# One core, cross attention with top-32 and a quantised feed-forward: the instruction order of all five engines written anew

## The chip, the core and the metric

The kernel runs on one NeuronCore of a Trainium2 chip. The metric is the device time of one execution in microseconds (us); less is better. The engines are named as in the profile: PE is TensorE (matmuls), PEld its weight loads, DVE is VectorE, ACT is ScalarE, POOL is GpSimd, and SP issues most of the DMAs. Each engine works through its own list of instructions in the order in which they are written and meets the others through semaphores alone, so an instruction that waits holds up all that stands behind it on its engine.

## What is computed

```python
x = x + xattn(layernorm(x), ctx_1024, top_k=32)       # x: 2048 x 256, ctx: 1601 x 256
x = x + ffn(layernorm(x))                             # 256 -> 1024 -> 256

# xattn: q = query @ Wq.T + bq;  k, v from ctx in the same way
scores = q @ k.T / sqrt(256)                          # 2048 x 1601
# all but the 32 largest scores of each row become -inf
ctx = softmax(scores) @ v;  out = ctx @ Wo.T + bo

# ffn: bitlinear, exact gelu, bitlinear
xq = act_quant(rmsnorm(x))    # rows to whole numbers -128..127, by the row's largest |x|
wq = weight_quant(w)          # -1, 0, 1, by the mean of |w|
h  = xq @ wq.T + b
```

## The kernel before

The 2048 rows are 16 tiles of 128, t = 0 to 15. Two neighbouring tiles form a pair, j = 0 to 7, and share a set of query transposes and quantisation scales. The 1601 context rows are cut into four column chunks c = 0 to 3 (400, 400, 400, 401) for the scores and into 13 blocks of 128 for the transposes; these blocks are handled in four groups q = 0 to 3 (4, 4, 4 and 1 blocks).

A head of about 43 us turns the context, folds the weight matrices together, projects keys and values, and makes the feed-forward weights ternary. Then each tile passes through these steps (names of the code's functions; each is one or a few instructions):

- PE `scores(t, c)`: 6 matmuls into PSUM bank `score<c>`; ACT `copy_scores(t, c)` copies it to `s_sb`. The four score banks exist once, so `scores(t+1, c)` waits for `copy_scores(t, c)`.
- DVE `candidates(t, c)` (8 MAX8 instructions), then `best_8` and three `next_8` (`drop_8` and `best_8`): the 32nd largest score. The first `best_8` also yields `neg_max`, on which ACT `exp_all(t)` waits. DVE `count(t)` tests whether the candidates suffice; SP `turn_counts(t)` brings its result into one row by DMA, DVE `largest_count(t)` reads it. DVE `weigh(t)` zeroes what is below the 32nd. `release(t)` reads the test's result in DVE's sequencer, branches, and gives the tile to PE.
- PE `turn_weights(t, q)` transposes into one of two banks (TURN), ACT `take_weights(t, q)` copies to `pT`, PE `weighted(t, q)` multiplies by the values. DVE `attended(t)` normalises and adds the residual, `moments(t)` and `centre(t)` are the second layer norm.
- POOL `row_scales_1(j)` (seven tiny steps) and `quantise_1(j, u)`, PE `turn_y1(j)`, ACT `take_y1(j)`, PE `up(t, h)` for the halves h = 0, 1, ACT `hidden(t, h)`, POOL `add_bias(t, h)`, ACT `gelu(t)` and `squares(t)`, DVE `gelu_max(t)`, POOL `row_scales_2(j)`, ACT `quantise_2(t)` and `lower_2(t)`, a transposing DMA `turn_y2(t)` on SP, PE `down(t)`, DVE `output(t)`, SP `store(t)`.

The last tiles go through variants of one tile or half a tile (`turn_y1_tile`, `gelu_half`, `tile_scales_1`, `tile_scales_2`, `quantise_half`) with DVE doing some of ACT's and POOL's steps; `hold_clock(23)` is 23 transposes whose result nobody reads. Tiles overlap: while PE does the attention of tile t, it also does scores of t+2 or t+3, `up` of the pair before and `down` of the one before that. ACT's exp and gelu need different function tables, and an ACT_TABLE_LOAD stands between them.

What sets the order is code written out by hand: each engine's body calls these functions one after another, in the middle of the kernel in a loop over rounds r (one pair each), so that every round has the same order. `s_sb`, `e_all`, `pT`, `cand` have two buffers (t modulo 2), x2 and cen four.

## Time and profile before

| | |
|---|---|
| device time, median of 3 runs | 279.48 us (278.39, 279.48, 279.64) |
| span of the profiled execution, first to last instruction | 277.2 us |
| median less span | 2.3 us |
| PE busy | 262.5 us (95%) |
| DVE busy | 230.2 us (83%) |
| ACT busy | 215.8 us (78%) |
| POOL busy | 165.0 us (60%) |
| PE idle from 42 to 219 us | 177.00 less 173.37: 3.6 us |
| PE idle from 219 us to the end | 58.2 less 48.7: 9.5 us |

The page gives no device time for the profiled execution itself; its span stands beside the runs' median. A busy time is the union of an engine's instructions. PE's matmuls overlap in the records (one lasts longer than the distance to the next), so PE's rate is read from the distances between starts, and a wait of 0.2 us is not seen as idle at all.

### The profile page before, as it was taken

The page shows a single profiled execution, that of the slowest core. Times are in us where ns is not written, and L with a number is a line of the kernel's source. Part 1 is how long each engine was busy: PE and PEld are TensorE (multiplying, and loading weights), DVE is VectorE, ACT ScalarE, POOL GpSimd, SP SyncE. Part 2 cuts the span into 40 slices and gives each one's busy share as a digit, 9 for nine tenths or more (in the row PEclk, how much of TensorE's full clock was granted, in tenths as well). Part 3 has the DMA queues.
Part 4 walks back from the last instruction along what each step waited for, and adds up shares of the span by engine and source line. Part 5 has one row for each costly group of instructions (what it writes and reads, how often), then busy time and mean ns, then how long its engine had stood idle before and what let it go on. Part 6 is the DMA issues. An engine that isn't in the chain of part 4 may idle for free. (4 is left out here: it accounts for less than half of the span.)

```text
span 277.2 us, 5366 instructions
## 1 busy us (share of the span) xinstructions
PE 262.5 (95%) x1527; PEld 230.4 (83%) x1527; DVE 230.2 (83%) x984; ACT 215.8 (78%) x323; POOL 165.0 (60%) x235
## 2 busy tenths in 40 slices
PE   7999999999999899999999999999999999799784
PEld 7999998998887788988898889888978898577463
DVE  2561868988979897989898989899989798989894
ACT  2567495586589988988799879987998899647762
POOL 3334409931888587849775887678767943612330
PEclk9999999999999999999999999999999999999999
DMA  6991010046000330025001500151004100610011
GB/s 223 316 342 40 4 38 0 1 79 151 2 2 0 77 78 0 0 69 125 0 4 45 139 5 4 38 140 18 0 1 124 31 1 2 151 38 5 0 38 38
DMA packets 29436, 16.42 MB, mean 59 GB/s; under 512 B 20445, under 2 KB 28190, under 8 KB 29406
## 3 DMA queue, kind: packets, MB, share of 16 engines
q1 hardware_dynamic: 28702, 15.02, 20.3%
q0 software_dynamic: 272, 0.79, 1.0%
q10 hardware_dynamic: 432, 0.26, 0.3%
q8 instruction: 12, 0.20, 0.3%
q14 instruction: 18, 0.15, 0.2%
HBM read 9.77 MB, written 2.10 MB: 43 GB/s over the span
## 5 line engine op out<-in xcount | busy, mean ns | idle before, releaser
L399 PE MATMUL bank<-vo,pT 128*128 128x257 f32 (+1 forms) x416 | 97.1, 381 | 2.4 <-ACT pT L1101 2.4
L399 PEld LDWEIGHTS bank<-vo,pT 128*128 128x128 f32 (+1 forms) x416 | 76.0, 190 | 15.1 <-ACT pT L1101 4.8
L1413 DVE MAX8 cand<-s_sb 128x8 f32<-128x50 f32 (+1 forms) x512 | 60.0, 201 | 1.6 <-issue 1.1
L258 PE MATMUL score<-k_high,q_low 128*128 128x400 f32 (+1 forms) x128 | 49.5, 387 | 0.0
L868 POOL TENSOR_TENSOR g<-g,b_bc 128x512 f32<-128x512 f32 x24 | 37.9, 1592 | 12.1 <-ACT g L1125 12.1
L258 PE MATMUL score<-k_low,q_high 128*128 128x400 f32 (+1 forms) x128 | 44.2, 346 | 0.0
L258 PE MATMUL score<-k_high,q_high 128*128 128x400 f32 (+1 forms) x128 | 44.0, 344 | 0.0
L1052 ACT ACTIVATE s_sb<-score 128x400 f32<-128x400 f32 x64 | 30.6, 504 | 10.2 <-PE score L258 10.1
L1101 ACT ACTIVATE pT<-bank 128x512 f32<-128x512 f32 x64 | 31.9, 514 | 4.2 <-PE bank L266 4.2
L1448 DVE SCALAR_TENSOR_TENSOR e_all<-s_sb,best,e_all 128x1601 f32<-128x1601 f32 x16 | 34.2, 2138 | 0.9 <-ACT e_all L1093 0.5
L266 PE MATMUL bank<-ident,e_all 128*128 128x128 f32 (+1 forms) x208 | 30.7, 273 | 2.6 <-ACT pT L1101 2.6
L1093 ACT ACTIVATE e_all<-s_sb,neg_max 128x1601 f32<-128x1601 f32 x16 | 26.1, 1629 | 4.5 <-DVE neg_max L1426 4.5
L266 PEld LDWEIGHTS bank<-ident,e_all 128*128 128x128 f32 (+1 forms) x208 | 24.4, 140 | 5.6 <-issue 3.6
L764 POOL TENSOR_SCALAR xn<-x_in,ln_mv,ln_r 128x256 f32<-128x256 f32 x16 | 27.8, 1741 | 0.9
L258 PEld LDWEIGHTS score<-k_high,q_low 128*128 128x128 f32 x128 | 24.1, 189 | 2.4
L258 PEld LDWEIGHTS score<-k_low,q_high 128*128 128x128 f32 x128 | 24.2, 189 | 0.7
L258 PEld LDWEIGHTS score<-k_high,q_high 128*128 128x128 f32 x128 | 24.1, 189 | 0.0
L1609 DVE TENSOR_REDUCE g_max<-g 128x1 f32<-128x1024 f32 x14 | 17.0, 1218 | 7.6 <-ACT g L1135 7.6
L1423 DVE MAX8 best<-cand 128x8 f32<-128x64 f32 (+1 forms) x64 | 20.8, 325 | 2.0
L822 POOL TENSOR_SCALAR row<-ln_mv 128x2 f32<-128x2 f32 x7 | 1.3, 192 | 28.8 <-issue 15.4
L1135 ACT ACTIVATE g<-g 128x1024 f32<-128x1024 f32 x14 | 14.9, 1067 | 3.7 <-POOL g L868 3.7
L1125 ACT ACTIVATE g<-bank,row 128x512 f32<-128x512 f32 x24 | 15.8, 685 | 2.3 <-PE bank L430 2.1
(162 smaller groups left out, 503.2 us busy)
## 6 DMA issues: line engine op xcount, KB each, us to landing
x_in<-in_x SPq DMA_DIRECT2D x16, 128.0 KB, 2.2
w_sb<-in_L_ffn_w SPq DMA_DIRECT2D x2, 1024.0 KB, 12.1
x_res<-in_x SPq DMA_DIRECT2D x16, 128.0 KB, 2.9
out<-o_sb SPq DMA_DIRECT2D x16, 128.0 KB, 2.0
ctx_sb<-in_ctx SPq DMA_DIRECT2D x2, 512.0 KB, 7.6
ctx_sb<-in_ctx SPq DMA_DIRECT2D x2, 256.0 KB, 4.1
b_bc<-in_L_ffn_b POOLq DMA_DIRECT2D x1, 512.0 KB, 7.6
w_q<-in_L_xattn_Wq SPq DMA_DIRECT2D x1, 256.0 KB, 2.8
```

The costliest lines, as they stand in the source:

```text
L258: ins = pe.matmul(out, a, b, start=(i == 0), stop=(i == len(steps) - 1))
L266: ins = pe.transpose(bank[0:src.shape[1], at:at + rows], src, ident[0:rows, 0:rows])
L399: ins = pe.matmul(bank[:, 0:DV], pT[0:n, t % 2, b * P:(b + 1) * P], vo[0:n, b, :], start=(b == 0), stop=(b == SB - 1))
L764: pool.tensor_scalar(xn[:, u, :], x_in[:, u, :], ln1_mv[:, u, 0:1], ln1_r[:, 1, u:u + 1], ALU.subtract, ALU.mult).then_inc(xn_ready, 1)
L868: pool.tensor_tensor(g[:, t % 2, part], g[:, t % 2, part], b1_bc[:, part], ALU.add).then_inc(biased, 1)
L1052: act.activation(s_sb[:, t % 2, at:at + n], score[c][:, 0:n], ACT.Copy).then_inc(s_copied, 1)
L1093: act.activation(e_all[:, t % 2, :], s_sb[:, t % 2, :], ACT.Exp, bias=neg_max[:, t % 2:t % 2 + 1], scale=SCALE).then_inc(e_ready, 1)
L1101: drain(act.activation(pT[0:rows, t % 2, lo * P:hi * P], bank(("p", t, q))[0:rows, 0:(hi - lo) * P], ACT.Copy), ("p", t, q))
L1413: ins = dve.max(cand[:, t % 2, k:CAND:PIECES], s_sb[:, t % 2, k * PIECE:end])
L1423: dve.max(best[:, u, k, :], cand[:, u, 0:DEPTH[k] * PIECES]).then_inc(topk_step[u], 1)
L1448: dve.scalar_tensor_tensor(e_all[:, u, :], s_sb[:, u, :], least_kept(t), e_all[:, u, :], ALU.is_ge, ALU.mult).then_inc(masked, 1)
L1609: dve.tensor_reduce(g_max[:, t % 2:t % 2 + 1], g[:, t % 2, :], AX.X, ALU.max, apply_absolute_value=True).then_inc(g_max_ready, 1)
```

## The change

The calls in the bodies of all five engines are put in another order. The loops over rounds are gone; each engine's calls are one flat list of some 60 to 400 lines, in which rounds differ from one another. No function is called more or less often, none on another engine, and the tiles, buffers and banks are the same. Three functions changed with it: `ternary`, `sum_weights` and `lower_weights` choose their tensor by number, `residual(0)` waits for the joined bias, and POOL's `quantise_1` waits for all seven steps of `row_scales_1` instead of standing right behind them.

```diff
-            for r in range(7):
-                if live(r - 1):
-                    turn_weights(2 * r - 1, 3)
...
+            turn_weights(11, 2)
+            turn_weights(11, 3)
+            scores(13, 2)
...
             def residual(t):
 
+                if t == 0:
+                    pool.wait_ge(bo_ready, 1)
                 pool.wait_ge(x_res_in[t % 2], (t // 2 + 1) * 16)
...
                 t = 2 * j + u
+                pool.wait_ge(row1_step, (j + 1) * ROW1)
                 if j:
                     wait_full(pool, ("y1", j - 1))
```

**ACT between two rounds.** `pT<-bank` is `take_weights`, `e_all<-s_sb,neg_max` is `exp_all`, `g_sq` is `squares`, `g<-g` is `gelu`, `s_sb<-score0` a score copy. Before, for tiles 11 and 12:

```order
L1101 ACTIVATE pT<-bank1 128x512
L1153 ACTIVATE g_sq,g_ssq<-g 128x1024
L1101 ACTIVATE pT<-bank0 128x512
L1093 ACT_TABLE_LOAD
L1093 ACTIVATE e_all<-s_sb,neg_max 128x1601
L1101 ACTIVATE pT<-bank1 128x512
L1052 ACTIVATE s_sb<-score0 128x400
L1052 ACTIVATE s_sb<-score1 128x400
L1101 ACTIVATE pT<-bank0 65x128
```

After, the same two tiles:

```order
L1315 ACTIVATE g<-g 128x1024
L1281 ACTIVATE pT<-bank0 128x512
L1333 ACTIVATE g_sq,g_ssq<-g 128x1024
L1281 ACTIVATE pT<-bank1 128x512
L1333 ACTIVATE g_sq,g_ssq<-g 128x1024
L1230 ACTIVATE s_sb<-score0 128x400
L1281 ACTIVATE pT<-bank0 65x128
L1273 ACT_TABLE_LOAD
L1273 ACTIVATE e_all<-s_sb,neg_max 128x1601
```

The third and fourth `take_weights` of tile 11 now stand ahead of the exp of tile 12 instead of behind it; the exp stands behind both `squares` and a score copy. There are 14 table loads in each program.

**PE near the end**, from the last chunk of scores, `scores(15, 3)` (its last matmul is the first row). `ident,e_all` is `turn_weights`, `w2T,y2T` is `down`, `vo,pT` is `weighted`, `ident,y1` is `turn_y1(6)`. Before:

```order
L258 MATMUL score3<-k_high,q_high 128x402
L454 MATMUL bank2<-w2T,y2T 128x256 x8
L266 MATMUL bank1<-ident,e_all 128x128 x4
L266 MATMUL bank0<-ident,e_all 128x128 x4
L266 MATMUL bank1<-ident,e_all 128x128 x4
L454 MATMUL bank3<-w2T,y2T 128x256 x8
L399 MATMUL bank2<-vo,pT 128x257 x4
L454 MATMUL bank3<-w2T,y2T 128x256 x8
L266 MATMUL bank0<-ident,y1 128x128 x4
L399 MATMUL bank2<-vo,pT 128x257 x4
```

After:

```order
L258 MATMUL score3<-k_high,q_high 128x402
L266 MATMUL bank1<-ident,e_all 128x128 x4
L266 MATMUL bank0<-ident,e_all 65x128
L454 MATMUL bank3<-w2T,y2T 128x256 x8
L266 MATMUL bank1<-ident,y1 128x128 x4
L399 MATMUL bank2<-vo,pT 128x257 x4
L430 MATMUL score0<-w1T,y1T 128x512 x2
L430 MATMUL score1<-w1T,y1T 128x512 x2
L399 MATMUL bank2<-vo,pT 128x257 x4
L454 MATMUL bank3<-w2T,y2T 128x256 x8
```

Two `turn_weights` of tile 14 and one `down` have moved ahead of these last scores, and `turn_y1(6)` now stands ahead of the first `weighted` of tile 14, where it stood behind it.

**DVE in the tail**, after the first output of the last group: `s_sb<-score,row1` is `hidden(15, h)`, `g_max` the maxima of tile 14 and 15, the five `row2` rows from `row2<-g_max,row2` on are `tile_scales_2(14)`. Before:

```order
L1632 SCALAR_TENSOR_TENSOR o_sb<-score0,row2,x2b 128x256
L1584 SCALAR_TENSOR_TENSOR s_sb<-score1,row1,b1_bc 128x512
L1584 SCALAR_TENSOR_TENSOR s_sb<-score2,row1,b1_bc 128x512
L1564 TENSOR_SCALAR row2<-g_ssq 128x1
L1632 SCALAR_TENSOR_TENSOR o_sb<-score3,row2,x2b 128x256
L1592 TENSOR_REDUCE g_max<-s_sb 128x1
L1530 SCALAR_TENSOR_TENSOR row2<-g_max,row2 128x1
```

After:

```order
L1941 SCALAR_TENSOR_TENSOR o_sb<-score3,row2,x2b 128x256
L1873 TENSOR_SCALAR row2<-g_ssq 128x1
L1901 TENSOR_REDUCE g_max<-s_sb 128x1 x2
L1839 SCALAR_TENSOR_TENSOR row2<-g_max,row2 128x1
L1840 TENSOR_SCALAR row2<-row2 128x1
L1841 RECIPROCAL row2<-row2 128x1
L1842 TENSOR_TENSOR row2<-row2 128x1
L1843 TENSOR_SCALAR row2<-row2,wmean 128x1
L1893 SCALAR_TENSOR_TENSOR s_sb<-score1,row1,b1_bc 128x512
L1893 SCALAR_TENSOR_TENSOR s_sb<-score2,row1,b1_bc 128x512
```

The maxima and scales of tile 14 have moved ahead of tile 15's hidden rows. On SP, `turn_counts(13)` stands behind `turn_y2(9)` in both; what is new is `load_residual(14)`, which waits for `attended(12)`, right ahead of it.

## Rows read from the trace of the kernel before

**Rows 1.** The page: busy time, share of the span and instructions

```profile
PE 262.5 (95%) x1527; PEld 230.4 (83%) x1527; DVE 230.2 (83%) x984; ACT 215.8 (78%) x323; POOL 165.0 (60%) x235
```

**Rows 2.** Chain from 204 to 217 us: start, us, what (back to back)

```profile
206.14 1.11 PE score L258 x6
...
208.12 0.87 PE bank L454 x8
208.99 0.87 PE bank L266 x8
209.86 3.48 PE bank L399 x16
...
216.08 0.45 PE bank L430 x2
```

**Rows 3.** Timeline of PE: start, us, instruction, [idle before it <- released by]

```profile
1.52 4.95 PE L462 MATMUL score<-ident 128*128 128x128 f32 x22 [1.52 <-POOL ident L739]
...
42.91 1.04 PE L266 MATMUL bank<-ident,e_all 128*128 128x128 f32 x8
...
201.40 1.90 PE L399 MATMUL bank<-vo,pT 128*128 128x257 f32 x8
203.69 2.44 PE L399 MATMUL bank<-vo,pT 128*128 128x257 f32 x10 [0.40 <-ACT pT L1101]
...
219.42 0.60 PE L430 MATMUL bank<-w1T,y1T 128*128 128x512 bf16 x2
```

**Rows 4.** Timeline of ACT, 200 to 231 us

```profile
200.23 1.28 ACT L1093 ACT_TABLE_LOAD   x1
...
203.06 0.58 ACT L1101 ACTIVATE pT<-bank 128x512 f32<-128x512 f32 x1
...
229.14 1.64 ACT L1093 ACTIVATE e_all<-s_sb,neg_max 128x1601 f32<-128x1601 f32 x1
```

**Rows 5.** Timeline of DVE, 206 to 258 us

```profile
206.74 0.17 DVE L1497 RECIPROCAL inv_sum<-bank 128x1 f32<-128x1 f32 x1 [0.69 <-PE bank L399]
...
208.87 0.99 DVE L1413 MAX8 cand<-s_sb 128x8 f32<-128x50 f32 x8
...
212.98 0.23 DVE L1423 MAX8 best<-cand 128x8 f32<-128x64 f32 x1
...
215.65 0.48 DVE L1455 SCALAR_TENSOR_TENSOR cand_ge<-cand,best,cand_worth 128x256 bf16<-128x256 f32 x1
...
223.24 2.78 DVE L1413 MAX8 cand<-s_sb 128x8 f32<-128x50 f32 x24
...
231.02 1.88 DVE L1448 SCALAR_TENSOR_TENSOR e_all<-s_sb,best,e_all 128x1601 f32<-128x1601 f32 x1
...
248.86 0.17 DVE L1497 RECIPROCAL inv_sum<-bank 128x1 f32<-128x1 f32 x1 [1.31 <-PE bank L399]
...
257.05 0.17 DVE L1497 RECIPROCAL inv_sum<-bank 128x1 f32<-128x1 f32 x1 [0.72 <-PE bank L399]
```

**Rows 6.** Timeline of POOL: the first step of `row_scales_1(5)`, and `quantise_1(5)`

```profile
209.10 0.19 POOL L822 TENSOR_SCALAR row<-ln_mv 128x2 f32<-128x2 f32 x1 [3.01 <-issue]
...
212.26 0.93 POOL L835 TENSOR_SCALAR y<-cen,row 128x256 f32<-128x256 f32 x2
```

**Rows 7.** The DMAs of line 628, `turn_counts`: issue in ns, then us to landing

```profile
L628 SPq DMA_DIRECT2D counts_row<-counts x16: 469/482/550, 37.3 to 244.3; - x16
...
DMA to landing us min/median/max: 1.9/1.9/2.0
```

**Rows 8.** Timeline of PE, 238 to 240 us

```profile
238.32 0.63 PE L266 MATMUL bank<-ident,e_all 128*128 128x128 f32 x4 [1.72 <-ACT pT L1101]
...
239.65 1.91 PE L399 MATMUL bank<-vo,pT 128*128 128x257 f32 x8
```

**Rows 9.** Timeline of DVE, 267 to 269 us: `tile_scales_2(14)` and the row behind its end

```profile
267.08 0.21 DVE L1530 SCALAR_TENSOR_TENSOR row<-g_max,row 128x1 f32<-128x1 f32 x1
...
268.03 0.14 DVE L1564 TENSOR_SCALAR row<-g_ssq 128x1 f32<-128x1 f32 x1
```

More of the change, by code:

```diff
@@ new lines, in _ @@
+            next_8(2, 2)
+            next_8(2, 3)
+            weigh(2)
+            attended(0)
+            count(2)
+            candidates(3, 0)
+            ln1_stats(4)
+            candidates(3, 1)
+            largest_count(2)
+            release(2)
+            candidates(3, 2)
+            moments(0)
+            candidates(3, 3)
+            centre(0)
+            attended(1)
+            moments(1)
+            best_8(3, 0)
+            centre(1)
+            next_8(3, 1)
+            next_8(3, 2)
@@ new lines, in _ @@
+            next_8(3, 3)
+            count(3)
+            largest_count(3)
+            attended(2)
+            moments(2)
+            weigh(3)
+            release(3)
+            candidates(4, 0)
+            candidates(4, 1)
+            centre(2)
+            candidates(4, 2)
+            gelu_max(0)
+            candidates(4, 3)
+            best_8(4, 0)
+            next_8(4, 1)
+            next_8(4, 2)
+            gelu_max(1)
+            next_8(4, 3)
+            count(4)
+            weigh(4)
@@ new lines, in _ @@
+            candidates(6, 0)
+            candidates(6, 1)
+            centre(4)
+            gelu_max(2)
+            candidates(6, 2)
+            candidates(6, 3)
+            gelu_max(3)
+            best_8(6, 0)
+            next_8(6, 1)
+            output(0)
+            next_8(6, 2)
+            next_8(6, 3)
+            count(6)
+            weigh(6)
+            largest_count(6)
+            release(6)
+            attended(5)
+            moments(5)
+            centre(5)
+            candidates(7, 0)
@@ new lines, in _ @@
+            candidates(7, 1)
+            candidates(7, 2)
+            candidates(7, 3)
+            output(1)
+            best_8(7, 0)
+            next_8(7, 1)
+            next_8(7, 2)
+            next_8(7, 3)
+            count(7)
+            attended(6)
+            weigh(7)
+            largest_count(7)
+            moments(6)
+            release(7)
+            ln1_stats(6)
+            output(2)
+            candidates(8, 0)
+            candidates(8, 1)
+            centre(6)
+            candidates(8, 2)
@@ new lines, in _ @@
+            candidates(8, 3)
+            gelu_max(4)
+            best_8(8, 0)
+            gelu_max(5)
+            next_8(8, 1)
+            next_8(8, 2)
+            next_8(8, 3)
+            candidates(9, 0)
+            count(8)
+            weigh(8)
+            output(3)
+            largest_count(8)
+            candidates(9, 1)
+            release(8)
+            attended(7)
+            moments(7)
+            centre(7)
+            candidates(9, 2)
+            candidates(9, 3)
+            ln1_stats(7)
@@ new lines, in _ @@
+            best_8(9, 0)
+            next_8(9, 1)
+            next_8(9, 2)
+            next_8(9, 3)
+            count(9)
+            weigh(9)
+            attended(8)
+            largest_count(9)
+            release(9)
+            candidates(10, 0)
+            candidates(10, 1)
+            candidates(10, 2)
+            output(4)
+            moments(8)
+            centre(8)
+            candidates(10, 3)
+            gelu_max(6)
+            best_8(10, 0)
+            next_8(10, 1)
@@ new lines, in _ @@
+            gelu_max(7)
+            next_8(10, 2)
+            next_8(10, 3)
+            count(10)
+            weigh(10)
+            largest_count(10)
+            release(10)
+            output(5)
+            attended(9)
+            moments(9)
+            centre(9)
+            candidates(11, 0)
+            candidates(11, 1)
+            candidates(11, 2)
+            candidates(11, 3)
+            best_8(11, 0)
+            next_8(11, 1)
+            next_8(11, 2)
+            next_8(11, 3)
@@ new lines, in _ @@
+            attended(10)
+            count(11)
+            weigh(11)
+            largest_count(11)
+            candidates(12, 0)
+            release(11)
+            candidates(12, 1)
+            output(6)
+            candidates(12, 2)
+            moments(10)
+            output(7)
+            gelu_max(8)
+            candidates(12, 3)
+            best_8(12, 0)
+            gelu_max(9)
+            next_8(12, 1)
+            next_8(12, 2)
+            next_8(12, 3)
+            count(12)
@@ L1774, in _ @@
             next_8(15, 3)
+            output(10)
+            count(15)
+            hidden(12, 0)
+            hidden(12, 1)
+            weigh(15)
             output(11)
[L1776 to L1778 removed]
             largest_count(15)
[L1780 removed]
             release(15)
```

990 lines of the change are left out of this document (644 added, 346 removed).

## The prediction

> **What bounds the kernel now.** I read the page's busy times first: PE 262.5 us of 277.2, DVE and ACT around 80% [rows 1]. Then the chain, for PE's pace where nothing holds it [rows 2]: a score matmul 1.11/6 = 0.183 us, a `down` matmul 0.109, a transpose 0.109, an instruction of `weighted` 3.48/16 = 0.2175 (two for each block), an `up` matmul 0.22. A round of one pair is 48 score matmuls (8.8), 26 transposes of weights (2.8), 52 of `weighted` (11.3), 8 of `up` (1.8), 16 of `down` (1.7) and 8 small transposes (0.9): 27.3 us. Then PE's timeline, where I take distances between starts. From the first weights' transpose (42.91) to the last `up` of tile 11 (219.42) [rows 3] the instructions at these paces make 169.6 us, and it takes 176.5: 6.9 us of waits in 6.3 rounds. So PE is the bound in the middle and loses little more than 1 us a round. The same count from the start gives 2.6 us of waits before 42.91, of which 1.52 is the wait for the identity [rows 3]. After 219 us the idle table shows 9.5 us; there DVE's chain for tiles 14 and 15 and then small steps in a line decide.
>
> **What a round waits for.** PE starts `weighted(11, 2)` 2.29 us after `weighted(11, 1)`, whose work is 8 x 0.2175 = 1.74 [rows 3]; 0.55 is a wait, and ACT shows why: it does the table load and the exp of tile 12, and only then, at 203.06, the copy that PE needs [rows 4]. This returns at tiles 3, 5, 7, 9 and, smaller, 13; with a start 0.1 slower behind each it makes 4.0 us of the 6.9.
>
> **What the change does to that.** In ACT's new order both copies stand ahead of that exp in rounds 11 and 5, and at tiles 3, 7, 9 and 13 PE's own order gives at least 5.1 us of other work between transpose and use, where 4.0 stood. I take the 4.0 us as gone, and of the other 2.9 (0.6 for a copy of tile 3, twice 0.5 ahead of query transposes, 0.15 a round on an `up` bank) nearly all, since each place now has other work.
>
> The new order sets two waits of its own. Between the last `weighted` of tile 3 and `turn_y1(1)` PE has 5.3 us of work, where 6.4 stood. In that time must come `attended`, `moments` and `centre`, 208.87 - 206.74 = 2.1 us [rows 5], POOL from the first scale to the end of both quantisations, 213.19 - 209.10 = 4.1 [rows 6], and the handover from DVE, 0.15: 6.4. I price it at 0.8, because just before it `release(4)` holds PE for another 0.8: the exp of tile 4 now has two `squares` ahead of it. With 0.1 for the rest, 1.7 us of waits stand where 6.9 did. PE also has 2.5 us more work ahead of the last `up` of tile 11 (12 more score matmuls 2.2, half a value projection 0.7, four transposes fewer -0.4) and 0.3 less ahead of its first weights' transpose. That `up` starts at 42.91 - 0.27 + 172.1 + 1.7 = 216.4 instead of 219.42: **-3.0**. The head itself I take at no gain: tile 0's first scores come some 5 us sooner, but their last chunk and all of tile 1 stand where they stood.
>
> **From there to `weigh(14)`.** Before, 231.02 - 219.42 = 11.6 [rows 3, 5]. ACT now has behind that `up` (0.44): hidden 0.58, table load 1.29, two gelus 1.92, three copies 1.44, a score copy 0.38, two `squares` 2.08, table load 1.30, exp 1.64 (distances in its timeline; the last is a row [rows 4]): 11.1. DVE comes to it through `weigh(13)`, two chunks of candidates, an output, the 32 best (215.65 - 212.98 = 2.7 [rows 5]), the count, two maxima, an output, moments, a chunk and `centre`. It would be ready with ACT, but for SP: `turn_counts(13)` stands behind a residual load that waits for `attended(12)`, so its result lands 0.5 + 0.5 + 1.9 = 2.9 us after that [rows 7], where `weigh(13)` fills 1.9. DVE waits some 0.8 more and arrives at 11.6 us behind the `up`. Still **-3.0** at `weigh(14)`: 228.0.
>
> **From `weigh(14)` to `attended(14)`.** Before 248.86 - 231.02 = 17.8 [rows 5]. DVE now: weigh and release 2.6, attended to centre 2.1 (232.7), three chunks 2.8 [rows 5], the best 2.7, an output and the count 0.8: 239.0. PE meanwhile stops at `turn_y1(6)`: centre of tile 13 at 232.7, the handover and POOL's 4.1 make 236.9, while PE's other work ends near 234.5. This is a new wait of some 2.4 us, and `weighted(14, 0)` is now queued behind it, but it still starts at 237.4 instead of 239.65 [rows 8]. From there PE has 1.74, two `up` 0.88, 1.74, `down` 0.87, 1.74 and 0.44, which puts `attended(14)` at 244.9; DVE's own line through `hidden(12)`, `weigh(15)` and `release(15)` ends at 244.0. That is 16.9 us: **-0.9**.
>
> **To `attended(15)`.** PE's work is 8.0 us against 8.19 before, where 0.5 was a wait: **-0.2**. It is at 252.9 instead of 257.05 [rows 5].
>
> **The tail.** Before 277.2 - 257.05 = 20.15 us. `turn_y1_tile(15)` now stands behind `down(12)`, and ACT takes `squares(14)` ahead of its copy: `up(15, 0)` comes 0.4 later. DVE does two maxima (1.2) and `tile_scales_2(14)`, 268.03 - 267.08 = 0.95 [rows 9], ahead of tile 15's hidden rows, which come 1.2 later after `attended(15)` than they did. At the end tile 14 is out of the way and 0.25 comes back: **+1.0**.
>
> The sum is -3.0 - 0.9 - 0.2 + 1.0 = -3.1. The profiled span goes from 277.2 to 274.1; the runs' median stands 2.3 above the span and I carry that over: **276.4 us**, 1.1% faster.
>
> **A rule weighed.** The table load in front of each exp takes 1.28 us [rows 4], and ACT's 11.1 us hold two. The Trainium skill (ScalarE: Activation LUTs, Rules for kernel authors) budgets about 2.7 us for every switch of set; the trace disagrees. By that figure the line would be an estimated 2.8 us longer, `weigh(14)` would wait for it, and the gain would nearly be gone; I go by the row.
>
> **The rivals.** A, as summed: -2 to -4.5. Chance 0.45.
>
> B: the waits that I priced don't come, because POOL's and DVE's steps overlap more than their distances tell. Without those at `turn_y1(1)`, `release(4)` and `turn_counts(13)` it is -2.1 more; without half of the tail's loss and with 0.8 from the head -1.3 more: -6.5, 273.0. For it speaks that many of PE's transposes stand within 0.5 us of when I reckon their input; against it, that such placing leaves nothing for chance. 0.20.
>
> C: the waits move instead of going. In each even round exp now stands behind `squares` and copies, and `release` comes only 0.3 to 1.1 us before PE's transpose by my reckoning (tiles 6, 10, 12). If each is 0.6 too late, five rounds give back 3.0: 279.4. 0.20.
>
> D, slower: the same line, from the odd tile's last `up` through gelus, `squares`, table load and exp to `release`, some 15 us, is longer than I add up. With a mean slack of 0.8 it eats the gain when it is 1.4 longer in each of five rounds; at 2.2 longer it is 5 x 1.4 = 7.0 of loss against 3.1: 283.4. For it: POOL's biases stand in this line too, and POOL now has residuals between them. Against it: ACT has 27 idle us of 177 in the middle. 0.10.
>
> E, slower: PE's clock falls in the new idle stretch of 2.4 us. The stretch of 1.72 before 238.32 left it up: four transposes and a `down` follow in 239.65 - 238.32 = 1.33 us, 12 x 0.109 being 1.31 [rows 8], the pace of 2.4 GHz. At the very start 22 transposes take 4.95 us [rows 3], twice that pace, as at 1.2 GHz. Four us of work at that price would make 280.4. The Trainium skill (TensorE: Matmul & The Clock Gate, Why this matters for your kernels) also says that idle gaps bring the half clock back; no gap inside this trace does. 0.05.
>
> **Range and chances.** A measurement tells 0.5%, 1.4 us, from no change. Faster by more: A, B and an edge of C, 0.66. Within: C, 0.20. Slower: D, E, little else, 0.14. The range reaches into B and over C: 271.5 to 280.0; A's own is 275.0 to 277.5.
>
> **What would show it.** No wait of PE for `pT` from tile 5 to 11; the last `up` of tile 11 at 216.4; a wait of about 0.8 ahead of `turn_y1(1)` and over 2 ahead of `turn_y1(6)`; `weigh(14)` at 228.0; `attended(15)` at 252.9; a tail of 21.1. Wrong would be PE waiting for `release` round after round, or a tail as short as before.

## The result, and the profile after

The changed kernel takes 296.3 us (median of 4; 295.5 to 298.1) against 279.4 (4 runs; 278.4 to 279.6): 1.063 times as long, with an interval of 1.059 to 1.067. 276.4 was predicted, and the range ended at 280.0. Its profiled execution has a span of 293.7 us where the other had 277.2, so 16.5 us are to be found.

The page of the changed kernel, the line that answers to [rows 1]:

```profile
PE 265.7 (90%) x1527; PEld 230.2 (78%) x1527; DVE 230.7 (79%) x984; ACT 217.1 (74%) x323; POOL 162.1 (55%) x235
```

DVE and ACT are busy for as long as before to within 1.3 us, POOL for 2.9 us less. PE's busy time is 3.2 us more, and the other 13.3 of the 16.5 are idle time on PE. The groups by line tell what PE waits for at L266, the transposes (busy us, mean ns | idle before, released by):

```profile
L266 PE MATMUL bank<-ident,e_all 128*128 128x128 f32 (+1 forms) x208 | 31.6, 278 | 11.5 <-DVEq L1796 10.7 <-ACT pT L1281 0.8
L266 PE MATMUL bank<-ident,y 128*128 128x128 f32 x28 | 4.5, 282 | 3.3 <-POOL y L993 3.2
```

L1796 is the last step of `release(t)`. PE waits 10.7 us for `release`, which it never did before. The waits for `pT` ahead of `weighted` (L399), which the change was to take away, are fewer but in sum as large (us in total, times, longest; the first row is of the kernel before):

```profile
PE bank L399 <- ACT pT L1101: 2.4, 5, 0.6
PE bank L399 <- ACT pT L1281: 2.3, 2, 1.4
```

The two that are left are at tiles 9 and 13. Such idle times are those of the profile. Where the prediction and the recorded expectations speak of a wait they take it from distances between starts, which gives 0.2 to 0.4 us more for the same place. For the stages I take the timeline at the places of the prediction's steps: PE at the first weights' transpose and the last `up` of tile 11 (to [rows 3]), then DVE at `weigh(14)`, `attended(14)` and `attended(15)` (to [rows 5]).

```profile
44.17 0.66 PE L266 MATMUL bank<-ident,e_all 128*128 128x128 f32 x4 [1.07 <-DVEq L1796]
...
235.34 0.61 PE L430 MATMUL bank<-w1T,y1T 128*128 128x512 bf16 x2
```

```profile
247.28 1.88 DVE L1757 SCALAR_TENSOR_TENSOR e_all<-s_sb,best,e_all 128x1601 f32<-128x1601 f32 x1
...
264.27 0.17 DVE L1806 RECIPROCAL inv_sum<-bank 128x1 f32<-128x1 f32 x1 [1.35 <-PE bank L399]
...
272.21 0.17 DVE L1806 RECIPROCAL inv_sum<-bank 128x1 f32<-128x1 f32 x1 [0.72 <-PE bank L399]
```

| stretch, us | before | predicted | after |
|---|---|---|---|
| start to first weights' transpose | 42.9 | 42.6 | 44.2 |
| from there to the last `up` of tile 11 | 176.5 | 173.8 | **191.2** |
| to `weigh(14)` | 11.6 | 11.6 | 11.9 |
| to `attended(14)` | 17.8 | 16.9 | 17.0 |
| to `attended(15)` | 8.2 | 8.0 | 7.9 |
| to the end | 20.2 | 21.1 | 21.5 |

One term holds nearly the whole error. A second division shows that two things are in it: `weigh(4)` starts at 90.4 before and at 99.3 after (+8.9); from `weigh(4)` to `weigh(14)`, five rounds, it is 140.6 and 147.95 (+7.4).

**The first piece: a load that stands in two queues.** DVE of the changed kernel, 51 to 60 us; L1757 is `weigh(1)`, L1663 `ln1_stats(3)`, L1722 the first chunks of `candidates(2, c)`, L1771 `largest_count(1)`:

```profile
51.02 1.88 DVE L1757 SCALAR_TENSOR_TENSOR e_all<-s_sb,best,e_all 128x1601 f32<-128x1601 f32 x1
57.09 0.75 DVE L1663 BATCH_NORM_STATS2 ln_part<-x_in 128x6 f32<-128x256 f32 x2 [4.19 <-DMA x_in<-in_x]
57.76 0.30 DVE L1666 BATCH_NORM_AGGREGATE ln_mv<-ln_part 128x2 f32<-128x6 f32 x2
57.98 1.86 DVE L1722 MAX8 cand<-s_sb 128x8 f32<-128x50 f32 x16
59.74 0.26 DVE L1771 TENSOR_REDUCE doubtful<-counts_row 1x1 int32<-1x128 f32 x1
```

SP at the same time: `turn_counts(1)`, a feed-forward weight's transposing DMA, and only then the load of x:

```profile
51.13 0.47 SPq L782 DMA_DIRECT2D counts_row<-counts  x1
51.64 2.07 SPq L789 DMA_TRANSPOSE w1T<-y  x1
53.77 1.43 SPq L771 DMA_DIRECT2D x_in<-in_x  x2
```

`load_x(3)` could have gone at 45.7, when POOL had used the buffer. On SP it stands behind `turn_counts(1)`, which waits for DVE. On DVE its reader stands ahead of `largest_count(1)`, whose own data had landed by 53.6. So `release(1)` waits for a load that it has nothing to do with. PE, 57 to 63 us (`turn_weights(1, 0)`, `turn_queries(2)`, `weighted(0, 3)`), and then its granted clock in stretches (busy us, PEclk, DMA share, GB/s):

```profile
60.97 1.12 PE L266 MATMUL bank<-ident,e_all 128*128 128x128 f32 x4 [3.76 <-DVEq L1796]
61.88 1.06 PE L266 MATMUL bank<-ident,xn 128*128 128x128 f32 x4
62.73 1.07 PE L399 MATMUL bank<-vo,pT 65*128 65x257 f32 x2
```

```profile
59.00:61.00 2.00, 0.03 (x1) 0.99 0.02 4
61.00:62.00 1.00, 1.00 (x5) 0.50 0.00 0
62.00:63.00 1.00, 1.00 (x6) 0.50 0.00 0
63.00:64.00 1.00, 1.00 (x4) 0.50 0.00 0
64.00:65.00 1.00, 1.00 (x6) 0.81 0.00 0
```

After 3.76 us of idleness PE works at half the clock (1.2 GHz) for 3.4 us: four transposes take 0.9 instead of 0.44. From 60.97 to 65.05 it does what takes 2.4 us at the full clock, so the wait costs 1.7 more than itself.

**The second piece: rounds of 29.6 us instead of 28.1.** I follow the work from `weigh(t)` to `weigh(t+2)`. In the kernel before each step starts as its input comes or as its engine has done what stands ahead of it. One walk of 27.8 us, the shortest of the five: `weigh(12)` 203.26, `attended(11)` 206.74, `centre(11)`, POOL's scales from 209.10, both `quantise_1(5)` from 212.26 [rows 5, 6], `turn_y1(5)` on PE, four `up` to 219.42 [rows 3], the biases, a gelu on ACT, the exp at 229.14 [rows 4], `weigh(14)` at 231.02 [rows 5]. The three of these rows that were not shown, from DVE, PE and ACT of the kernel before:

```profile
203.26 1.89 DVE L1448 SCALAR_TENSOR_TENSOR e_all<-s_sb,best,e_all 128x1601 f32<-128x1601 f32 x1
```

```profile
213.29 0.61 PE L266 MATMUL bank<-ident,y 128*128 128x128 f32 x4
```

```profile
221.01 1.06 ACT L1135 ACTIVATE g<-g 128x1024 f32<-128x1024 f32 x1 [0.28 <-POOL g L868]
```

The quantised rows end at 213.19 and PE takes them at 213.29; the bias ends at 220.98 and the gelu starts at 221.01. From `turn_y1(5)` the walk goes over the `up` of the pair's first tile (from 215.92), its hidden rows and its two biases to the gelu (POOL, three biases in one row):

```profile
217.40 4.83 POOL L868 TENSOR_TENSOR g<-g,b_bc 128x512 f32<-128x512 f32 x3 [0.67 <-ACT g L1125]
```

The last `up` (219.42) is only a landmark: it is not an input of that gelu, so the links ahead of it and behind it have to be read together. Along this walk no step has slack, in any of the five rounds. Its links, worked out from the starts (of the gelu: the first of its pair), all in us:

| link | before, t = 10 | after, t = 4 | 6 | 8 | 10 | 12 | sum of five, after less before |
|---|---|---|---|---|---|---|---|
| `weigh(t)` to `attended(t-1)` | 3.49 | 3.11 | 3.80 | 3.62 | 4.55 | 4.33 | +1.8 |
| to the end of `quantise_1` | 6.45 | 6.44 | 6.44 | 6.43 | 6.44 | 6.41 | -0.1 |
| to `turn_y1` | 0.09 | 0.05 | 0.06 | 0.46 | 1.06 | 0.05 | +1.3 |
| to the last `up` | 6.28 | 6.17 | 7.20 | 6.43 | 4.38 | 6.19 | -0.9 |
| to the gelu | 1.97 | 2.73 | 1.24 | 2.71 | 3.65 | 2.72 | +3.4 |
| to the exp of t + 2 | 8.12 | 9.34 | 9.36 | 7.30 | 8.75 | 7.25 | +1.4 |
| to `weigh(t+2)` | 1.74 | 2.09 | 1.74 | 1.74 | 1.73 | 1.97 | +0.5 |
| round | 28.13 | 29.95 | 29.82 | 28.67 | 30.57 | 28.93 | +7.4 |

The two links around the last `up` together make +2.5. At the prediction's paces PE's own work in a round is 27.3 us before (26.4 in the first of the five) and 27.2 as a mean after, where single rounds have 25.1 to 28.2. One round of after, t = 10, read where it got longer. POOL: `normalise(7, 1)` (L918, 3.03 us) stands ahead of `add_bias(8, h)` (L1026), while `hidden(8, 0)` was there at 203.2:

```profile
201.93 3.03 POOL L918 TENSOR_SCALAR xn<-x_in,ln_mv,ln_r 128x256 f32<-128x256 f32 x1
204.94 2.51 POOL L1026 TENSOR_TENSOR g<-g,b_bc 128x512 f32<-128x512 f32 x2
```

ACT: the first gelu, then the end of the line, where a score copy and the last `pT` copy stand ahead of the table load:

```profile
207.87 1.06 ACT L1315 ACTIVATE g<-g 128x1024 f32<-128x1024 f32 x1
...
213.61 1.05 ACT L1333 ACTIVATE g_sq<-g 128x1024 bf16<-128x1024 f32 x1
214.56 0.20 ACT L1333 ACTIVATION_READ_ACCUMULATOR g_sq<-g 128x1 f32 x1
214.65 0.50 ACT L1230 ACTIVATE s_sb<-score 128x400 f32<-128x400 f32 x1
215.03 0.27 ACT L1281 ACTIVATE pT<-bank 65x128 f32<-65x128 f32 x1
215.32 1.28 ACT L1273 ACT_TABLE_LOAD   x1
216.62 1.63 ACT L1273 ACTIVATE e_all<-s_sb,neg_max 128x1601 f32<-128x1601 f32 x1
```

### The profile page after: what moved, and what is told of

The parts are those of the page before. It is cut to its first block and busy times, and to the rows that moved or that the text cites. A ratio compares the mean times of both kernels' runs of the same rounds, so it can differ in the third digit from the quotient of the medians.

```text
span 293.7 us, 5378 instructions
## 1 busy us (share of the span) xinstructions
PE 265.7 (90%) x1527; PEld 230.2 (78%) x1527; DVE 230.7 (79%) x984; ACT 217.1 (74%) x323; POOL 162.1 (55%) x235
## 5 line engine op out<-in xcount | busy, mean ns | idle before, releaser
L399 PE MATMUL bank<-vo,pT 128*128 128x257 f32 (+1 forms) x416 | 98.7, 382 | 2.3 <-ACT pT L1281 2.3
L399 PEld LDWEIGHTS bank<-vo,pT 128*128 128x128 f32 (+1 forms) x416 | 76.4, 190 | 13.2 <-ACT pT L1281 3.4
L1722 DVE MAX8 cand<-s_sb 128x8 f32<-128x50 f32 (+1 forms) x512 | 61.0, 202 | 7.2 <-ACT s_sb L1230 4.6
L258 PE MATMUL score<-k_high,q_low 128*128 128x400 f32 (+1 forms) x128 | 50.5, 394 | 0.0
L266 PE MATMUL bank<-ident,e_all 128*128 128x128 f32 (+1 forms) x208 | 31.6, 278 | 11.5 <-DVEq L1796 10.7
L1026 POOL TENSOR_TENSOR g<-g,b_bc 128x512 f32<-128x512 f32 x24 | 34.7, 1458 | 8.6 <-ACT g L1305 8.6
L266 PEld LDWEIGHTS bank<-ident,e_all 128*128 128x128 f32 (+1 forms) x208 | 24.6, 142 | 18.1 <-DVEq L1796 14.0
L1757 DVE SCALAR_TENSOR_TENSOR e_all<-s_sb,best,e_all 128x1601 f32<-128x1601 f32 x16 | 32.0, 1999 | 4.5 <-ACT e_all L1273 4.5
L918 POOL TENSOR_SCALAR xn<-x_in,ln_mv,ln_r 128x256 f32<-128x256 f32 x16 | 21.5, 1346 | 9.9 <-PE bank L266 9.6
L1341 ACT ACTIVATE y_raised<-g,magic_col,row 128x1024 f32<-128x1024 f32 x14 | 17.2, 1237 | 2.0 <-POOL row L1048 2.0
L1004 POOL TENSOR_TENSOR x2b<-x,b_bc 128x256 f32<-128x256 f32 x16 | 14.8, 933 | 4.9 <-DVE x L1808 4.3
L1918 DVE TENSOR_REDUCE g_max<-g 128x1 f32<-128x1024 f32 x14 | 16.9, 1210 | 0.7 <-ACT g L1315 0.7
```

Source lines behind the costliest of these rows:

```text
L258: ins = pe.matmul(out, a, b, start=(i == 0), stop=(i == len(steps) - 1))
L266: ins = pe.transpose(bank[0:src.shape[1], at:at + rows], src, ident[0:rows, 0:rows])
L399: ins = pe.matmul(bank[:, 0:DV], pT[0:n, t % 2, b * P:(b + 1) * P], vo[0:n, b, :], start=(b == 0), stop=(b == SB - 1))
L918: pool.tensor_scalar(xn[:, u, :], x_in[:, u, :], ln1_mv[:, u, 0:1], ln1_r[:, 1, u:u + 1], ALU.subtract, ALU.mult).then_inc(xn_ready, 1)
L1026: pool.tensor_tensor(g[:, t % 2, part], g[:, t % 2, part], b1_bc[:, part], ALU.add).then_inc(biased, 1)
L1341: act.activation(y2_raised[:, t % 2, :], g[:, t % 2, :], ACT.Identity, scale=row2[:, j % 2, 5, t % 2:t % 2 + 1], bias=magic_col[:, 0:1]).t ...
```

## The experiments

Lines with a minus or a plus are calls that leave or come; "..." stands for the calls in between. The kernel before took 278.8 to 279.8 (medians) beside these runs.

**Head and rest apart.** `head_of_after`: all engines do first what the changed kernel had begun by 72.8 us, in its order, then the rest in the order of before.

> The other way round: first what the changed kernel had begun by 72.8 us, in the new order, then the rest in the order of before. If head and middle are separate: 279.4 + 8 = about 287. If before's middle can make up for a late start: 280 to 283. If the head were not the matter: 279.

286.6 us, 1.030 times the kernel before (1.025 to 1.035). `weigh(4)` starts at 97.9 where it started at 90.4; from there to `weigh(14)` it takes 140.1, behind that 46.2, as in the kernel before (140.6 and 46.2). So the new head costs 7.5 us and the old middle gives back 0.5 at most; the new middle and tail cost the other 9.7.

`head_of_before`, the other way round.

> All five engines do first what the kernel before had begun by 66.5 us (to turn_weights(2, 0)), in the order of before, and then the rest in the new order. PE's stalls in the changed kernel add up to 10.9 us at turn_weights(2, 0), in the one before to about 2.9. If the loss of the head and that of the middle are separate, it takes 8 off the 296.3: about 288. Rival 1: the middle's waits are only the head's lateness handed on, then it comes near 280. Rival 2: the head's loss is made up behind it anyway, then it stays above 295.

299.0 us. The number is that of the second rival, but the run says nothing for it, because the join had made a stall of its own: DVE's `ln1_stats(4)` waits 4.95 us for its load, `turn_y1(0)` on PE waits 7.15, and PE's clock is halved (granted 0.50) until 87.5 us. `head_of_before_2` was to mend that:

```diff
             candidates(3, 0)
-            ln1_stats(4)
             candidates(3, 1)
...
             count(3)
+            ln1_stats(4)
```

> head_of_before again (the old head, the new rest), with ln1_stats(4) on DVE behind count(3): in head_of_before it stood between two chunks of candidates(3), waited 4.95 us for the load of x and left PE idle for 7.2 us, which the join of the two orders had made. Old head plus new middle and tail should be the kernel before plus the 9.7 us by which the changed kernel (296.3) exceeds head_of_after (286.6): 288.8. A second stall at the join would show as more.

298.1 us, again not the 288.8 expected. On POOL `normalise_scale(4)` stands ahead of `row_scales_1(0)`, so the wait only changed engines, and PE waits 8.39 us. As sums both say nothing. But behind the join `weigh(4)` to `weigh(14)` takes 147.5 us with another head and another start, as in the changed kernel (147.95), and 150.0 in `head_of_before`: the long rounds belong to the new order of the middle.

**The head's load.** `dve_release1_first`:

```diff
             weigh(1)
+            largest_count(1)
+            release(1)
             ln1_stats(3)
             candidates(2, 0)
             candidates(2, 1)
-            largest_count(1)
             candidates(2, 2)
-            release(1)
```

> The changed kernel with one move on DVE: largest_count(1) and release(1) ahead of ln1_stats(3), candidates(2, 0) to (2, 2). In the trace DVE waits 4.2 us in ln1_stats(3) for the load of x, while the counts of tile 1 had landed by 53.6 us; release(1) would come at about 55 instead of 60.9, before PE asks for it at 57.2. The theory that this order costs the 3.9 us of stall at turn_weights(1, 0) expects 292.4. The rival, that the next release (tile 2, whose candidates still stand behind the load) takes the wait over, expects over 295.

297.5 us, no gain. The release comes at about 55 as wanted and PE does not wait at 57.7, but the candidates of tile 2 still wait for the load, with them the exp of tile 2, and behind that exp on ACT stands the copy of `turn_weights(1, 0)`: PE waits 4.84 us at `turn_weights(1, 1)`. The rival that another wait takes this one over had the mechanism, one engine further. `sp_load3_first` moves the load itself:

```diff
+            load_x(3)
             turn_counts(1)
             turn_ffn_weights(0)
-            load_x(3)
```

> The changed kernel with one move on SP: load_x(3) ahead of turn_counts(1) and turn_ffn_weights(0), DVE as it is. Its input was free at 45.7 us, it was issued at 53.8. The theory that SP's queue holds DVE: ln1_stats(3) starts at 52.9 with no wait, largest_count(1) at 55.6, release(1) at 56.8, candidates of tile 2 some 4 us sooner: PE's 3.9 us at turn_weights(1, 0) go and part of the 1.2 at turn_weights(2, 0): 291.5 to 292.5. The rival, that DVE has too much work ahead of release(1) in any case, expects over 295.

291.9 us (289.7 to 292.7), as expected. DVE no longer waits, and `largest_count(1)` stands where it was computed:

```profile
51.25 1.88 DVE L1757 SCALAR_TENSOR_TENSOR e_all<-s_sb,best,e_all 128x1601 f32<-128x1601 f32 x1
53.05 0.74 DVE L1663 BATCH_NORM_STATS2 ln_part<-x_in 128x6 f32<-128x256 f32 x2
53.71 0.30 DVE L1666 BATCH_NORM_AGGREGATE ln_mv<-ln_part 128x2 f32<-128x6 f32 x2
53.93 1.86 DVE L1722 MAX8 cand<-s_sb 128x8 f32<-128x50 f32 x16
55.70 0.26 DVE L1771 TENSOR_REDUCE doubtful<-counts_row 1x1 int32<-1x128 f32 x1
```

`head3_of_after`, the same move in `head_of_after`:

> The kernel of head_of_after (286.6: the new head, the old rest) with load_x(3) ahead of turn_counts(1) in the new head. If the 4.4 that this move took from the changed kernel belong to the head alone: 282.2.

282.7 us. The move is worth 4.4 in one kernel and 3.9 in the other (5.1 and 5.4 by the ratios to the kernel before that ran beside each), so it belongs to the head. It is not the whole of it: 282.7 is still 2.9 above the 279.8 beside it, and `weigh(4)` starts at 94.1 instead of 90.4. No run tells what makes up this rest.

**What bounds the middle of the kernel before.** `before_pe_work` adds work on PE alone, in the places where it waited for `pT`:

```diff
+                if c == 1 and t in (5, 7, 9, 11, 13):
+                    for _ in range(3):
+                        pe.matmul(score[c][:, 0:n], q_low[:, 0, qs], k_high[:, 0, cols], start=True, stop=True)
```

> The kernel before with work added on PE alone: three more score matmuls (0.55 us, the result is overwritten by the product that follows) ahead of scores(t, 1) for t = 5, 7, 9, 11, 13, so 2.75 us more for PE in the middle. Theory L: a round of 28.1 us is not set by PE's 27.3 but by a loop through all engines (weigh, attended, centre, POOL's scales, turn_y1, up, biases, gelu, squares, exp, weigh), and PE's waits for pT are its slack: then the added work goes into these waits, and the time stays within 0.5 of 279.1. The prediction's view, that PE bounds the middle and each us on PE counts: 281.8.

279.1 us beside 279.8, ratio 0.998 (0.996 to 0.9995). PE does 2.75 us more and nothing gets longer; `weigh(4)` to `weigh(14)` is 140.62. The idle times ahead of `weighted` at tiles 5, 7, 9 and 11 (0.54, 0.39, 0.40 and 0.40 us before) are gone: the added work lies in them. `before_pe_work_9`, nine matmuls in each place:

> As before_pe_work, with nine extra score matmuls (1.65 us) in each of the five places, 8.25 us in all. PE's own work is then 27.3 + 1.65 = 28.95 us a round, 0.8 more than the loop's 28.14: theory L expects a bend, 5 x 0.8 = 4.0 longer than the kernel before, 283.2. If PE's slack were not in these rounds at all, 8 longer.

281.8 us, 1.010 (1.007 to 1.012): 8.25 us of work cost 2.9. The bend is there. The rounds go 28.1, 28.6, 28.8, 28.9, 29.0: the first ones still live on what slack there was, which I had left out. `before_copies_first` takes the prediction's own term, on ACT, for the odd tiles 3 to 13:

```diff
+            take_weights(11, 2)
             exp_all(12)
-            take_weights(11, 2)
```

> The kernel before with six moves on ACT and nothing else: take_weights(t, 2) ahead of exp_all(t+1) for t = 3, 5, 7, 9, 11, 13. It takes one term of the prediction by itself: PE's stalls of 0.75, 0.63, 0.66, 0.48, 0.48 and 0.30 at weighted(t, 2) go, and exp comes 0.48 later, where release of tile t+1 had 1.1 to spare. By the prediction's step 279.4 - 3.3 = 276.1. The rival, that the later exp pushes release past PE's turn_weights(t+1, 0), expects 278 or more.

281.7 us, 1.010 (1.007 to 1.012), slower by 2.6. The waits for `pT` ahead of `weighted` are gone in its trace, and in each round PE waits ahead of the next tile's first transpose instead, here at `turn_weights(12, 0)`:

```profile
208.75 1.09 PE L266 MATMUL bank<-ident,e_all 128*128 128x128 f32 x8 [0.60 <-DVEq L1796]
```

The link from gelu to exp went from 8.12 to 8.62, and the five rounds from 140.6 to 143.5: 5 x 0.5, and 0.4 elsewhere. What is added to the loop is added to the round. The same trace settles another doubt. In the kernel before the profile puts DVE's 0.69 us ahead of `attended(11)` [rows 5] down to PE's product, which would put PE's wait for `pT` on the loop. Here that product is made some 2 us ahead of `attended(11)`, and the gap stays (DVE):

```profile
208.95 0.17 DVE L1806 RECIPROCAL inv_sum<-bank 128x1 f32<-128x1 f32 x1 [0.70 <-issue]
```

From `weigh(12)` to `attended(11)` it is 3.48 us in both. So `release` in DVE's sequencer fills this gap, and PE's product is not what DVE waits for.

**Repairs of the new middle**, all on top of `sp_load3_first` (291.9, 1.044 times the kernel before beside it, 1.039 to 1.050). They ran beside executions of the kernel before with medians of 278.9 to 279.8, so the ratios to it stand with them. `sp_counts_first`, on SP:

```diff
+            turn_ffn_weights(1)
             load_x(4)
-            turn_ffn_weights(1)
...
+            turn_y2(1)
             load_x(5)
-            turn_y2(1)
+            turn_counts(5)
             load_residual(6)
-            turn_counts(5)
...
+            turn_counts(13)
             load_residual(14)
-            turn_counts(13)
```

> The changed kernel with load_x(3) first, as in sp_load3_first (291.9), and four more moves on SP: turn_ffn_weights(1) ahead of load_x(4), turn_y2(1) ahead of load_x(5), turn_counts(5) ahead of load_residual(6), turn_counts(13) ahead of load_residual(14). In the trace the counts of tiles 2, 5 and 13 were sent 1.0, 1.2 and 2.2 us after they were there. PE's stalls behind them are 0.45, 0.99 and 0.35, and weigh(13) is late anyway: about 1.4 off, 290.5. The rival, that SP's queue sets all releases by its DMA traffic, expects 288 or less; the rival that DVE is late in these rounds anyway expects 291.9.

291.8 us, ratio 1.046. `turn_weights(5, 0)` no longer waits, `turn_weights(6, 0)` waits 1.95 instead of 1.25, and PE's clock is halved behind it, from 128.1 to 131.6. The time is that of the rival that DVE is late anyway.

`act_exp_first`, on ACT; the exps of tiles 12 and 14 move like that of tile 4, `take_weights(1, 0)` and `(13, 3)` like `(9, 3)`:

```diff
+            exp_all(4)
             squares(1)
-            exp_all(4)
...
+            take_weights(9, 3)
             quantise_2(6)
...
-            take_weights(9, 3)
```

> The kernel of sp_load3_first (291.9) with six moves on ACT: exp_all(4), (12) and (14) ahead of the second squares of their round, take_weights(1, 0) ahead of exp_all(2), take_weights(9, 3) ahead of quantise_2(6), take_weights(13, 3) ahead of quantise_2(10). PE's stalls at these places are 1.65 (tile 4), 1.18 (tile 12), 1.03 (tile 1), 1.74 (tile 9), 1.20 (tile 13), and 1.7 of half clock behind the one at tile 4. If ACT's order alone makes them: 1.1, 0.9, 0.9, 1.7, 1.1 and the 1.7 go, 7 in all, 285. If each only hands on to the step behind it (POOL's scales behind squares, the quantised rows, DVE), 2 or less goes: 290.

296.8 us, ratio 1.063 (1.060 to 1.066), 5 slower. The exp of tile 4 came 1.0 sooner, but `squares(1)` later, POOL's scales with it, and ACT then stands in `quantise_2(0)`, ahead of the copy that PE needs (ACT, then PE):

```profile
97.49 1.24 ACT L1341 ACTIVATE y_raised<-g,magic_col,row 128x1024 f32<-128x1024 f32 x1 [3.34 <-POOL row L1048]
```

```profile
101.33 1.08 PE L266 MATMUL bank<-ident,e_all 128*128 128x128 f32 x4 [4.16 <-ACT pT L1281]
```

PE's clock is halved behind this wait (granted 0.50 from 101 to 106), and behind a second one of 3.74 us for `pT` in the tail, at 254.

`sp_and_act` has all lines of both diffs.

> Both sets of moves. If the two are separate, the gains against 291.9 add up: 283.6 when both come as computed. If DVE's own line is the next bound in the same rounds, it is hardly better than act_exp_first alone.

298.0 us, ratio 1.067 (1.064 to 1.071), like `act_exp_first` alone.

`after_loop_moves`, on ACT (tile 12's; tiles 4, 6 and 8 alike) and on DVE:

```diff
             squares(9)
+            exp_all(12)
             copy_scores(13, 0)
             take_weights(11, 3)
-            exp_all(12)
...
-            candidates(13, 1)
             attended(11)
             moments(11)
             centre(11)
+            candidates(13, 1)
```

> The kernel of sp_load3_first (291.9) with moves that shorten the loop of theory L: on ACT exp_all(4), (6), (8), (12) ahead of the copies that the new order had put in front of it (0.48, 0.64, 0.92 and 0.54 us; the squares stay ahead of exp, other than in act_exp_first), on DVE attended(11), moments(11), centre(11) ahead of candidates(13, 1) (0.9). The loop's rounds get shorter by the sum, 3.5, less what becomes tied elsewhere: 288.4 to 290. By the prediction's view these copies then keep PE waiting again for pT and nothing is gained: 291.5 or more.

294.0 us, 2 slower, but with a ratio of 1.050 (1.047 to 1.054) not clear of the 1.044. The links from gelu to the exps of tiles 8 and 12 fell as computed, by 0.9 and 0.5. But in the new order `candidates(13, 0)` stands ahead of `weigh(12)` on DVE, and its score copy now stood behind the exp. From the exp to `weigh(12)` it went from 1.7 to 3.7, and to `weigh(8)` from 1.7 to 3.5 (DVE, tile 12):

```profile
214.35 1.00 DVE L1722 MAX8 cand<-s_sb 128x8 f32<-128x50 f32 x8 [2.40 <-ACT s_sb L1230]
215.27 0.34 DVE L1823 TENSOR_SCALAR cen<-x,ln_mv 128x256 f32<-128x256 f32 x1
215.64 0.42 DVE L1825 TENSOR_REDUCE cen_max<-cen 128x1 f32<-128x256 f32 x1
215.98 2.69 DVE L1757 SCALAR_TENSOR_TENSOR e_all<-s_sb,best,e_all 128x1601 f32<-128x1601 f32 x1
```

`after_pool_bias_first`, on POOL:

```diff
-            normalise(7, 1)
             add_bias(8, 0)
             add_bias(8, 1)
+            normalise(7, 1)
```

> The kernel of sp_load3_first (291.9) with one move on POOL: normalise(7, 1) behind add_bias(8, 1). In that trace hidden(8, 0) ends at 198.76, and add_bias(8, 0) starts at 200.47, because normalise(7, 1) (3.0 us, beside a weigh on DVE) stands ahead of it. This link of the loop (last up to gelu) took 3.6 us in that round against 2.0 in the kernel before. Theory L: 1.3 us off this round and off the end, 290.6. Rival: it is PE's order that sets this round, nothing changes.

292.5 us, ratio 1.047. The time to the end of the bias fell by 1.3, and the time from there to the gelu grew by 1.3: ACT has a copy, `hidden(9, 1)` and another copy ahead of the gelu. In the traced execution (293.8) PE's clock is also halved from 188.8 to 192, which makes this round 1.5 longer at `turn_y1(4)`; that lies ahead of the moved call.

`after_bias_and_gelu` adds, on ACT, and alike for `gelu(6)` and `gelu(10)`:

```diff
+            gelu(8)
             hidden(9, 1)
             copy_scores(12, 2)
-            gelu(8)
```

> The same with three more moves, on ACT: gelu(6) ahead of hidden(7, 1), gelu(8) ahead of hidden(9, 1), gelu(10) ahead of copy_scores(14, 3), as the kernel before has them. The table load then lies in the wait for the biases. The links from the last up to gelu are 2.71, 3.64 and 2.73 us there against 1.95, 1.97 and 1.59 before: with the POOL move up to 3.5 off, 288.4. Where DVE or the candidates' copies are tied within 1 us, half of it: 290.

292.0 us, ratio 1.046. The round from t = 8 is 1.1 shorter (27.55), as computed. The next is 1.2 longer: with `gelu(8)` ahead of it, `hidden(9, 1)` empties its bank later, and `down(7)` on PE waits 1.88 us for that bank. So none of these six kernels gained anything.

**The tail of the kernel before.** `before_tail_moves`, on ACT and on PE:

```diff
+            take_weights(14, 0)
+            take_weights(14, 1)
             lower_2(11)
...
-            down(11)
             turn_y1(6)
             weighted(14, 1)
+            down(11)
```

> The kernel before with three moves near the end: take_weights(14, 0) and (14, 1) on ACT ahead of lower_2(11), and on PE down(11) behind weighted(14, 1). PE's stall of 2.08 at turn_weights(14, 2) is there because take_weights(14, 0) stands behind lower_2(11) (1.15 us), and behind 231 us PE sets attended(14) and (15). Expect 1.0 less, 278.1. The rival, that the next step (turn_y1(6), whose rows come from POOL) takes it over: 279.

282.4 us beside 279.8, 1.013 (1.008 to 1.019). `take_weights(14, 0)` came sooner, but `output(11)` stands ahead of `count(15)` on DVE and waited 2.79 us for the `down(11)` that I had moved back.

`before_tail_2` keeps the move on ACT; on PE and on DVE:

```diff
+            weighted(14, 1)
             down(11)
             turn_y1(6)
-            weighted(14, 1)
...
             weigh(15)
+            largest_count(15)
+            release(15)
             hidden(12, 0)
-            largest_count(15)
             hidden(12, 1)
-            release(15)
```

> The kernel before with the end's moves mended after before_tail_moves, where down(11), put later, held output(11), count(15) and weigh(15) on DVE. Now down(11) keeps its place behind turn_y2 and weighted(14, 1) goes ahead of it, into the wait; take_weights(14, 0) and (14, 1) stay ahead of lower_2(11); on DVE largest_count(15) and release(15) go ahead of hidden(12, 0) and (12, 1). attended(14) then waits for DVE at about 247.7 instead of PE at 248.86, turn_weights(15, 0) comes 0.5 to 1.1 sooner: 278.2 by the kernel before's 279.1, 0.3% less. Rival: output(11) waits for down(11) again and it is slower.

282.3 us, 1.009 (1.006 to 1.013). `attended(14)` came 0.2 us later behind `weigh(14)` than before, and then PE stood idle 2.49 us at `turn_weights(15, 2)` instead of 0.48: the copies of tile 15 stand behind `gelu(12)`, whose inputs `hidden(12, h)` I had put behind the release. The ten executions fall into two groups. Three have a granted clock of 1.000 and take 279.6 to 279.8 us; seven have 0.992 to 0.994 and take 282.0 to 283.1. The traced one is of the second group, and its clock is halved from 251.8, right behind that wait, to 255.2. So most of the loss is the clock's price for the new gap, and the order alone is within about 1 us of the kernel before. No kernel tried beats the one before, other than `before_pe_work` by 0.2%, which is less than the medians of the kernel before differ among these groups of runs (278.8 to 279.8).

## Why the prediction was wrong

- **"PE is the bound in the middle"** failed, and what failed in the middle hangs on it; the head's loss is a matter of its own. PE's 27.3 us are the largest busy time of a round, but the round was 28.14 because of the loop. 2.75 us more work on PE cost nothing.
- **"I take the 4.0 us as gone"** is the step of the sum that failed. The waits for `pT` at tiles 3, 5, 7 and 11 did go, but those at tiles 9 and 13 grew, to 1.7 and 1.2 by the prediction's measure; the 5.1 us of other work that I had counted there did not cover the fourth copy, which stands behind `quantise_2` on ACT. And the old ones had been slack: `before_copies_first`, which takes them away by the move of the copy alone, is 2.6 us slower. The two copies ahead of exp, which I had counted for the change, lie in the longest link.
- **"1.7 us of waits stand where 6.9 did."** By the same count, 191.2 less 172.1 of work, it was 19.1. Of the two waits that I priced, `turn_y1(1)` came as priced, 0.7 (0.8), and `release(4)` came twice as long, 1.66 (0.8). What I left out was the 3.8 us in the head, with the half clock behind it, and every other round.
- **"The head itself I take at no gain", and no loss.** It lost 7.5. I had compared PE's positions only, and read SP's queue at `turn_counts(13)` alone. The same reading at `load_x(3)` would have shown its 4 us.
- **C** named what happened in kind, waits that move to `release`, and "PE waiting for `release`" was my sign of being wrong. PE is idle ahead of `release` nine times, 10.7 us in all. Of C's own places tiles 6 and 12 have 0.7 each and tile 10 has none; the large ones are elsewhere, so 3.0 us was far too little.
- **D** had the right mechanism, a line from the last `up` through gelus, table load and exp to `release` that is longer than the copies it saves, at a chance of 0.10. I asked whether the line is longer than PE's work; it was already equal to the round, so every us on it counted from the first. The five rounds alone are 7.4 longer, where nearly all of the -3.0 was forecast for them, so they are some 10 off; D gave them 7.0. Which links made them longer is read from the trace and not shown by a run.
- **E** held in part. I looked at one gap of 2.4 us; the fall came behind the gap of 3.76 that I had not foreseen, for 1.7 us. The Trainium skill (TensorE: Matmul & The Clock Gate, Why this matters for your kernels) says that idle gaps bring the half clock back; this trace agrees (granted 0.50 behind the 3.76), where that of the kernel before, whose longest gap inside is 1.72 us, had no such place.
- **Behind `weigh(14)` the working held,** and a short forecast that comes out there says nothing for the mechanism ahead of it. To `attended(14)` 17.0 (16.9), to `attended(15)` 7.9 (8.0), tail 21.5 (21.1), and the new wait ahead of `turn_y1(6)`:

```profile
256.18 0.66 PE L266 MATMUL bank<-ident,y 128*128 128x128 f32 x4 [2.06 <-POOL y L993]
```

What stays open: the rest of the head's loss, about 3 us behind the load's, and the price of each link in the new middle. The table reads them from the trace, and the old middle's dependence on the loop is shown by three kernels, but no removal of one link shortened the new middle as a whole. The three stalls that replaced them are read from traces. Nor was an order tried in which all five engines are repaired together.

## What to carry to other kernels

In a kernel whose rounds repeat, measure the period and walk from one instruction to the same one a round later, through whichever engine released it: if that walk has no slack, it is the bound, even where an engine is 95% busy, and that engine's short waits can be its slack and not a gain to be had, as the 2.75 us of free work showed here. Adding work on the suspected engine is a cheap test of it. And where several in-order lists are fitted to each other, a call moved in one list must be checked against what stands behind it there and against who reads its result on the others; ask first of each DMA whether the wait ahead of it in its queue is its own.
